# Two stacked attention layers on one core: self attention scores on two 64-row halves with keys spread over half as many columns, value products that alternate between two batches, passes written out

## The chip, the cores and the metric

The kernel runs on one core of one Trainium2 chip. The metric is the device time of one execution in microseconds (us); less is better. Engines are named as in the profile: PE is the matrix engine (PEld its loading of the stationary operand), DVE the vector engine, ACT the scalar engine, POOL the GpSimd engine, SP the engine that issues the transfers. They run side by side and wait for one another on semaphores.

## What is computed

Thirty-two batches of 56 tokens with 128 channels go through two layers. The first has self attention with 16 heads of 8 channels, a cross attention over 1500 context tokens, and an MLP; the second has self attention with 16 heads of 64 channels, and a gated MLP. The change touches the first layer's self attention alone:

```python
def _forward(tgt, src, ...):                 # first layer, T = 56, C = 128, H = 16, HD = 8
    scale = C ** (-0.5)
    x = _layernorm(tgt, ln1_g, ln1_b)
    qkv = x @ sa_wqkv
    q, k, v = (_heads(t) for t in jnp.split(qkv, 3, axis=-1))
    wei = jnp.einsum('bhtd,bhsd->bhts', q, k) * scale
    wei = jnp.where(causal[None, None], wei, NEG_INF)
    wei = jnp.where(tgt_padding_mask[:, None, None, :], NEG_INF, wei)
    wei = jax.nn.softmax(wei, axis=-1)
    sa_out = _merge(jnp.einsum('bhts,bhsd->bhtd', wei, v)) @ sa_wproj + sa_bproj
    result = tgt + sa_out
    ...                                      # cross attention on layernorm(result)
    h = jax.nn.relu(_layernorm(tgt, ln3_g, ln3_b) @ ff_w1 + ff_b1)
    return result + (h @ ff_w2 + ff_b2)
```

## The kernel before

The kernel is one program of three blocks, one behind the other: the self attention of the first layer with its MLP (to about 204 us), the cross attention (to about 970 us), and the second layer. All engines meet at the end of a block. In the first block two batches lie on the 128 partitions, 64 rows each (56 tokens and 8 empty rows): a pair. Sixteen pairs are worked off in four passes of `U = 4` pairs. The passes are a loop that each engine runs for itself (`Fori(0, NIT)`, lines 346, 432, 477 and 539); a wait in it counts semaphores up by the pass, which takes register instructions on the engine.

Within a pass:

- ACT copies the normed inputs to `xn_now` (L434), PE makes queries and keys of all four pairs (L350, L351), the values (L357, two batches by turns on the two halves of the output rows) and the up projection of the MLP (L364); ACT copies the keys to `k0` (L436) and the scaled queries to `q0` (L437), and does the MLP's rectifier (L440).
- Heads have only 8 channels. So that one product makes the scores of many heads, the keys are spread out: `k_wide[u]` has, for each batch of the pair, a column block of 64 keys for each of the 16 heads, and in it the rows of other heads are zero. It is `k0` times `own_head`, a table of ones and zeros, 128x1024 for each batch. DVE makes those of pairs 0 and 1 (L547), POOL those of pairs 2 and 3 (L484). The fourth pair uses the buffer of the first, so POOL waits for the first pair's scores (L481, L482) before it; the third pair uses the buffer `z`, that of the layer norm's rows.
- PE makes the scores of a pair with four products (L379): all 128 rows of the contraction, a batch's 64 queries as the stationary operand, 512 columns of `k_wide`. The two batches go to the two halves of the output rows. The third and fourth pair wait until the maximum over the pair two before is out (`s0_max`), since they use its PSUM banks.
- DVE adds the mask (L559) and takes the maximum (L561), POOL subtracts it (L491), ACT takes the exponential (L445), and DVE the sums (L564). Before the mask add stands the wide form of the values (L553) on DVE.
- PE makes the down projection (L387) ahead of the first transposes of the exponentials (L397); ACT copies the transposed halves to `e0_t` (L451), and `values0` (L325 to L336) multiplies with the values: 16 products for a pair, 8 of the first batch and then 8 of the second, each with 64 stationary columns and 16 moving ones (L330).
- DVE multiplies with the reciprocal sums (L573), PE transposes (L406) and projects (L410), and DVE adds to the residual (L579, L580).

Behind the passes come a layer norm of the result and the queries of the cross attention in two 16-bit parts (`q_halves`, which lies in the buffer of `k_wide[0]`; L587, L589).

## Time and profile before

| | us |
|---|---|
| median of 3 runs | 1343.94 (1338.87 to 1344.26) |
| the profiled execution | 1345.08 |
| its span, first to last instruction | 1343.3 |
| PE busy | 1169.8 (87% of the span) |
| DVE busy | 928.7 (69%) |
| POOL busy | 847.5 (63%) |
| ACT busy | 747.0 (56%) |

Busy shares are means over stages that differ in what bounds them; they say little about one stage.
### The profile page before, as it was taken

How to read it: one execution, taken by the hardware profiler on the slowest of the kernel's cores; microseconds unless marked ns; L12 is line 12 of the kernel's file. 1: busy time of each engine (PE TensorE's matmuls, PEld its weight loads, DVE VectorE, ACT ScalarE, POOL GpSimd, SP SyncE). 2: the span in 40 equal slices, each digit the busy share in tenths (PEclk: the TensorE clock that was granted, in tenths of full speed). 3: DMA queues.
4: the chain of work that ended last, by engine and by line, in shares of the span. 5: the costliest groups of instructions: out<-in, count | busy, mean ns of one | idle time of the engine just before them, and what ended most of it. 6: DMA issues, size and time to landing. Idle time of an engine off the chain costs nothing. (4 is left out here: it accounts for less than half of the span.)

```text
span 1343.3 us, 38339 instructions
## 1 busy us (share of the span) xinstructions
PE 1169.8 (87%) x15980; PEld 795.3 (59%) x15980; DVE 928.7 (69%) x1742; ACT 747.0 (56%) x1029; POOL 847.5 (63%) x1227
## 2 busy tenths in 40 slices
PE   3888855899999999999999999998766887879775
PEld 2555544566666666666666666665443746456472
DVE  6778764777777777778787878777266375674632
ACT  2333333477777777777777777776512435344251
POOL 2455538878787878787888888851028294572830
PEclk9999866899999999999999999999877888989885
DMA  6200003323232323232223232211000000000000
GB/s 170 70 0 0 0 0 108 119 69 107 83 107 69 119 72 114 77 102 89 100 77 112 79 104 86 71 60 37 4 14 1 1 1 10 0 8 2 8 2 7
DMA packets 70398, 75.88 MB, mean 56 GB/s; under 512 B 21308, under 2 KB 64956, under 8 KB 70108
## 3 DMA queue, kind: packets, MB, share of 16 engines
q1 hardware_dynamic: 70236, 73.57, 17.3%
q8 instruction: 120, 1.97, 0.6%
q14 instruction: 42, 0.34, 0.1%
HBM read 32.90 MB, written 0.92 MB: 25 GB/s over the span
## 5 line engine op out<-in xcount | busy, mean ns | idle before, releaser
L928 DVE TENSOR_REDUCE tops_sb<-ps_b 112x2 f32<-112x1000 f32 x384 | 460.4, 1199 | 158.4 <-PE ps_b L778 155.7
L874 ACT ACTIVATE probs_sb<-ps_a 128x896 f32<-128x896 f32 x352 | 322.7, 917 | 118.5 <-PE ps_a L759 118.5
L750 PE MATMUL ps_d<-probs_sb,values_sb 128*32 128x112 f32 x6144 | 229.1, 267 | 0.6 <-ACT probs_sb L874 0.5
L778 PE MATMUL ps_b<-keys_sb,queries_sb 64*112 64x500 f16 x768 | 164.8, 420 | 16.6 <-DVE tops_sb L928 9.8
L217 POOL TENSOR_SCALAR context_sb<-context_sb,ln_sb 125x128 f32<-125x128 f32 x384 | 166.2, 449 | 7.6 <-POOL ln_sb L235 7.5
L750 PEld LDWEIGHTS ps_d<-probs_sb,values_sb 128*32 128x32 f32 x6144 | 135.5, 110 | 40.3 <-issue 7.5
L759 PEld LDWEIGHTS ps_a<-queries_sb,keys_sb 64*128 64x128 f16 x3072 | 125.2, 102 | 48.8 <-ACT probs_sb L874 8.1
L759 PE MATMUL ps_a<-queries_sb,keys_sb 64*128 64x112 f16 x3072 | 141.2, 210 | 4.7 <-ACT probs_sb L874 4.1
L806 PE MATMUL ps_c<-xs_t_sb,w_kv_sb 128*128 128x200 f32 (+1 forms) x384 | 127.4, 430 | 0.0
L815 PE MATMUL ps_c<-w_kv_sb,xs_t_sb 128*128 128x128 f32 x768 | 122.0, 297 | 5.1 <-ACT k_rows_sb L891 5.1
L815 PEld LDWEIGHTS ps_c<-w_kv_sb,xs_t_sb 128*128 128x128 f32 x768 | 97.9, 195 | 27.5 <-issue 21.9
L693 POOL TENSOR_TENSOR k_split_sb<-k_rows_sb,k_split_sb 128x500 f16<-128x500 f32 x96 | 108.8, 1134 | 8.0
L1094 POOL TENSOR_TENSOR turn_b_sb<-turn_b_sb,const_sb 128x448 f32<-128x448 f32 x64 | 62.9, 983 | 75.9 <-DVE turn_b_sb L1429 75.9
L778 PEld LDWEIGHTS ps_b<-keys_sb,queries_sb 64*112 64x112 f16 x768 | 50.6, 126 | 95.7 <-DVE tops_sb L928 70.4
L691 POOL CAST k_split_sb<-k_rows_sb 128x500 f16<-128x500 f32 x96 | 57.5, 599 | 57.8 <-ACT k_rows_sb L891 57.7
L965 DVE BATCH_NORM_STATS2 st_sb<-context_sb 125x6 f32<-125x128 f32 x372 | 87.5, 279 | 2.0 <-POOL ln_sb L235 2.0
L903 ACT ACTIVATE xs_t_sb<-ps_c,cols_sb 128x500 f32<-128x500 f32 x96 | 73.7, 767 | 18.5 <-PE ps_c L828 18.4
L806 PEld LDWEIGHTS ps_c<-xs_t_sb,w_kv_sb 128*128 128x128 f32 x384 | 61.4, 196 | 26.1 <-issue 23.4
L891 ACT COPY k_rows_sb<-ps_c 128x500 f32<-128x500 f32 x96 | 55.3, 576 | 37.9 <-PE ps_c L806 28.2
L233 POOL TENSOR_TENSOR ln_sb<-ln_sb,power_sb 125x12 f32<-125x12 f32 x32 | 72.9, 2279 | 2.5
L206 POOL TENSOR_TENSOR sums_sb<-context_sb 125x768 f32<-125x768 f32 x32 | 58.1, 1817 | 24.4 <-PE ps_d L860 24.4
L896 ACT COPY values_sb<-ps_c 128x512 f32<-128x512 f32 x96 | 56.2, 585 | 29.7 <-PE ps_c L815 29.2
(258 smaller groups left out, 1949.9 us busy)
## 6 DMA issues: line engine op xcount, KB each, us to landing
keys_sb<-k_split_sb SPq DMA_DIRECT2D x288, 125.0 KB, 2.5
context_sb<-in_ctx SPq DMA_DIRECT2D x32, 750.0 KB
queries_sb<-q_split_sb SPq DMA_DIRECT2D x24, 112.0 KB, 5.6
keys_sb<-in_ones SPq DMA_DIRECT2D x3, 375.0 KB, 4.5
w_qk_sb<-in_w_qkv SPq DMA_DIRECT2D x1, 1024.0 KB, 12.3
queries_sb<-shift_sb SPq DMA_DIRECT2D x64, 1.8 KB
x_all_sb<-in_x SPq DMA_DIRECT2D x2, 448.0 KB
queries_sb<-in_zeros SPq DMA_DIRECT2D x8, 112.0 KB, 5.5
```

Source lines behind the costliest of these rows:

```text
L217: ins = nc.gpsimd.tensor_scalar(tile, tile, ln[:, 4, k:k + 1], ln[:, 5, k:k + 1], ALU.mult, ALU.add)
L233: link(nc.gpsimd.tensor_tensor(rstd, var, power[:].broadcast_to([KP, KT]), ALU.pow))
L693: nc.gpsimd.tensor_tensor(k_split[:, 1, k_slice], k_rows[(b + u) % 2][:], k_split[:, 0, k_slice], ALU.subtract).then_inc(Q["klow_ready"], 1)
L750: last = nc.tensor.matmul(o_bank[32 * (g % 4):32 * (g % 4) + 32, 112 * (g // 4):112 * (g // 4) + 112], values[r][:, k, g, :], probs[k % 2] ...
L759: last = nc.tensor.matmul(ps_a[:, 512 * e + GN * g:512 * e + GN * g + GN], keys[r][64 * e:64 * e + 64, g, KEY * k:KEY * k + KEY], queries_ ...
L778: last = nc.tensor.matmul(ps_b[0:2 * T, 512 * e:512 * e + 500], queries_of(b + d, e, g), keys[(r + d) % 3][64 * e:64 * e + 64, g, 500 * u: ...
L806: last = nc.tensor.matmul(ring_of(b, u)[:, lo:hi], w_kv[:, 0:128], xs_t[:, 500 * u + lo:500 * u + hi], start=True, stop=True)
L815: last = nc.tensor.matmul(ring_of(b, 3 + u)[:, 128 * k:128 * k + 128], xs_t[:, 4 * KEY * u + KEY * k:4 * KEY * u + KEY * k + KEY], w_kv[:, ...
L874: nc.scalar.activation(probs[s % 2][:].rearrange("p (e n) -> p e n", e=2), halves(ps_a[:, :]), ACT.Exp).then_inc(Q["probs_ready"], 1)
L903: nc.scalar.activation(xs_t[:, 500 * u:500 * u + 500], ring_of(b, 6 + u)[:, 0:500], ACT.Identity, bias=cols[:, 3:4], scale=cols[:, 2:3]).t ...
L928: nc.vector.tensor_reduce(tops[(b + d) % 2][:, :, n // 3, n % 3], ps_b[0:2 * T, :].rearrange("p (e n) -> p e n", e=2)[:, :, 0:500], axis=A ...
L965: ins = nc.vector.bn_stats(st[:, k, :], context[(r + 1) % 3][:, k, :])
```

## The change

The 128 rows of the contraction hold 16 heads of 8 channels, so the upper 64 rows hold heads 0 to 7 and the lower 64 rows heads 8 to 15. Now a score product contracts over 64 rows only, and a column block of `k_wide` serves two heads: head h in the upper half of the rows and head h + 8 in the lower half. `own_head` and `k_wide` have 8 column blocks instead of 16. A pair still has four products of 512 columns; the first half's go to the first PSUM bank, the second half's to the second, as the heads did before.

The buffers that were shared are now separate: four `k_wide`, and `q_halves`. With that POOL's wait for the first scores goes. In `values0` the loop over the two batches is inside that over the head groups. The passes are Python loops now, so each engine's four passes are written out and the waits compare with constants.

```diff
-    own_head = (p[:, None] // D0 == np.arange(H0)[None]).astype(np.float32)
+    own_head = (p[:, None] % 64 // D0 == np.arange(H0 // 2)[None]).astype(np.float32)
...
-            k_bufs = [sb1(f"k_wide{n}", [128, 2, H0, TP])[:] for n in range(2)]
-            k_bufs.append(z[:].rearrange("p n c -> p (n c)").rearrange("p (b h s) -> p b h s", b=2, h=H0))
-            k_wide = [k_bufs[n] for n in (0, 1, 2, 0)]
+            k_wide = [sb1(f"k_wide{n}", [128, 2, H0 // 2, TP]) for n in range(U)]
...
-            q_halves = k_bufs[0].rearrange("p b h s -> p (b h s)").bitcast(F16).rearrange(
-                "p (q a n) -> p q a n", q=NPAIR // U, a=2)
+            q_halves = sb1("q_halves", [128, NPAIR // U, 2, U * 128], F16)
...
                     def values0(pe, i, u):
...
-                        for b2 in range(2):
-                            for c in range(8):
+                        for c in range(8):
+                            for b2 in range(2):
                                 last = nc.tensor.matmul(banks[0][64 * b2:64 * b2 + 64, 128 * u + 16 * c:128 * u + 16 * c + 16],
...
-                    with pe.Fori(0, NIT) as i:
+                    for i in range(NIT):
...
-                            for half in range(2):
-                                for b2 in range(2):
+                            for b2 in range(2):
+                                for half in range(2):
+                                    rows = slice(64 * half, 64 * half + 64)
                                     last = nc.tensor.matmul(ps[64 * b2:64 * b2 + 64, 512 * half:512 * half + 512],
-                                                            q0[:, 128 * u + 64 * b2:128 * u + 64 * b2 + 64],
-                                                            k_wide[u][:, b2, 8 * half:8 * half + 8, :].rearrange("p h s -> p (h s)"),
+                                                            q0[rows, 128 * u + 64 * b2:128 * u + 64 * b2 + 64],
+                                                            k_wide[u][rows, b2, :, :].rearrange("p h s -> p (h s)"),
                                                             start=True, stop=True)
...
                         for u in (2, 3):
-                            if u == 3:
-                                wait("s0_done", 1)
                             for b2 in range(2):
                                 ins = nc.gpsimd.tensor_tensor(
                                     k_wide[u][:, b2, :, :],
-                                    k0[:, 128 * u + 64 * b2:128 * u + 64 * b2 + 64].unsqueeze(1).broadcast_to([128, H0, TP]),
-                                    own_head.unsqueeze(2).broadcast_to([128, H0, TP]), ALU.mult)
+                                    k0[:, 128 * u + 64 * b2:128 * u + 64 * b2 + 64].unsqueeze(1).broadcast_to([128, H0 // 2, TP]),
+                                    own_head.unsqueeze(2).broadcast_to([128, H0 // 2, TP]), ALU.mult)
...
```

DVE's product at L547 changes in the same way, and the loops of ACT, POOL and DVE as PE's.

What stands on POOL in a pass before, from the wide keys of pairs 2 and 3 (written to `z` and `k_wide`) to the first subtraction of the maximum (`s_0`):

```order
L484 ISA
L484 TENSOR_TENSOR z_sb<-k_sb,const_sb 128x1024 [waits self_k0_ready]
L484 TENSOR_TENSOR z_sb<-k_sb,const_sb 128x1024
L283 ISA
L484 TENSOR_TENSOR k_wide_sb<-k_sb,const_sb 128x1024 [waits self_s0_done]
L484 TENSOR_TENSOR k_wide_sb<-k_sb,const_sb 128x1024
L491 TENSOR_TENSOR s_0_sb<-s_0_sb,s_max_sb 128x1024 [waits self_s0_max]
```

And the same place now:

```order
L480 ISA
L480 TENSOR_TENSOR k_wide_sb<-k_sb,const_sb 128x512 [waits self_k0_ready,x_loaded]
L480 TENSOR_TENSOR k_wide_sb<-k_sb,const_sb 128x512 x3
L487 TENSOR_TENSOR s_0_sb<-s_0_sb,s_max_sb 128x1024 [waits self_s0_max]
```

The four products stand in one row without a wait between them, each half as wide, and the register instructions are gone.

On PE, the scores of the first three pairs before (`self_k_ready` and `self_k_later` are the wide keys of DVE and POOL, `self_up_ready` the rectifier on ACT):

```order
L283 ISA [waits self_q0_ready]
L379 MATMUL ps_a<-k_wide_sb,q_sb 64x512 [waits self_k_ready]
L379 MATMUL ps_a<-k_wide_sb,q_sb 64x512 x3
L283 REGISTER_ALU
L283 REGISTER_ALU [waits self_k_ready]
L379 MATMUL ps_c<-k_wide_sb,q_sb 64x512 [waits self_up_ready]
L379 MATMUL ps_c<-k_wide_sb,q_sb 64x512 x3
L379 MATMUL ps_a<-z_sb,q_sb 64x512 [waits self_s0_max,self_k_later]
```

And now:

```order
L377 MATMUL ps_a<-k_wide_sb,q_sb 64x512 [waits self_k_ready,self_q0_ready]
L377 MATMUL ps_a<-k_wide_sb,q_sb 64x512 x3
L377 MATMUL ps_c<-k_wide_sb,q_sb 64x512 [waits self_up_ready,self_k_ready]
L377 MATMUL ps_c<-k_wide_sb,q_sb 64x512 x3
L377 MATMUL ps_a<-k_wide_sb,q_sb 64x512 [waits self_s0_max,self_k_later]
```

As many products stand there, in the same place and with the same waits; they contract over half as many rows, and the third pair's keys no longer lie in `z`.

## Rows read from the trace of the kernel before

**Rows 1.** Stretch of the third pass: start:end, length, busy time (records) by engine, PEclk, DMA

```profile
100.80:138.70 37.90, 32.95 (x280) 21.92 (x280) 27.79 (x24) 13.64 (x21) 18.01 (x8) 0.95 0.00 0
```

**Rows 2.** Timeline (start, duration, engine, line, operation, [idle before <-releaser]): block's end

```profile
202.86 1.09 DVE L589 TENSOR_TENSOR q_split_sb<-k_wide_sb,const_sb 128x896 f16<-128x896 f16 x1
...
204.47 0.37 PE L860 MATMUL ps_d<-ones_sb,sums_sb 125*128 125x1 f32 x1 [5.65 <-DVE xs_t_sb L909]
```

**Rows 3.** Timelines of DVE and POOL, third pass, wide keys one by one

```profile
105.97 1.23 DVE L547 TENSOR_TENSOR k_wide_sb<-k_sb,const_sb 128x1024 f32<-128x1024 f32 x1 [1.44 <-ACT k_sb L436]
106.01 2.94 POOL L484 TENSOR_TENSOR z_sb<-k_sb,const_sb 128x1024 f32<-128x1024 f32 x1 [17.24 <-ACT k_sb L436]
107.11 2.92 DVE L547 TENSOR_TENSOR k_wide_sb<-k_sb,const_sb 128x1024 f32<-128x1024 f32 x1
...
112.80 1.21 DVE L547 TENSOR_TENSOR k_wide_sb<-k_sb,const_sb 128x1024 f32<-128x1024 f32 x1
112.99 2.78 POOL L484 TENSOR_TENSOR k_wide_sb<-k_sb,const_sb 128x1024 f32<-128x1024 f32 x1 [1.20 <-PE ps_a L379]
```

**Rows 4.** Two lines' instructions: count, ns min/median/max, first and last start us

```profile
L567 DVE TENSOR_TENSOR r_sb<-x_all_sb,rows_sb x4: 691/692/869, 54.2 to 169.4; 128x512 f32 x4
...
L1094 POOL TENSOR_TENSOR turn_b_sb<-turn_b_sb,const_sb x64: 973/982/993, 999.5 to 1267.0; 128x448 f32<-128x448 f32 x64
```

**Rows 5.** Timeline of PE, third pass, up projection to value products

```profile
107.14 3.89 PE L364 MATMUL ps_c<-xn_now_sb,w_up_sb 128*128 128x512 f32 x8
110.96 1.94 PE L379 MATMUL ps_a<-k_wide_sb,q_sb 128*64 128x512 f32 x8
...
120.06 1.94 PE L379 MATMUL ps_c<-k_wide_sb,q_sb 128*64 128x512 f32 x8 [0.45 <-DVE s_max_sb L561]
...
125.60 0.60 PE L397 MATMUL ps_b<-const_sb,s_sb 128*128 128x128 f32 x4
...
130.22 0.60 PE L397 MATMUL ps_d<-const_sb,s_sb 128*128 128x128 f32 x4
130.75 1.83 PE L330 MATMUL ps_a<-v_wide_sb,e_t_sb 128*64 128x16 f32 x32
132.51 0.66 PE L397 MATMUL ps_b<-const_sb,s_sb 128*128 128x128 f32 x4
...
133.53 3.29 PE L330 MATMUL ps_a<-v_wide_sb,e_t_sb 128*64 128x16 f32 x64
```

**Rows 6.** Timeline of DVE, third pass: first mask add, last sum, normalising

```profile
115.07 1.21 DVE L559 TENSOR_TENSOR s_sb<-ps_a,mask_sb 128x1024 f32<-128x1024 f32 x1
...
128.30 1.22 DVE L564 TENSOR_REDUCE s_sum_sb<-s_sb 128x16 f32<-128x1024 f32 x1 [0.24 <-ACT s_sb L445]
...
136.85 0.69 DVE L573 TENSOR_TENSOR q_sb<-ps_a,s_sum_sb 128x512 f32<-128x512 f32 x1 [4.44 <-PE ps_a L330]
```

**Rows 7.** Timelines of POOL and ACT, third pass, around the fourth exponential

```profile
124.76 1.91 POOL L491 TENSOR_TENSOR s_sb<-s_sb,s_max_sb 128x1024 f32<-128x1024 f32 x1 [0.48 <-DVE s_max_sb L561]
...
126.24 0.58 ACT L451 COPY e_t_sb<-ps_b 128x512 f32<-128x512 f32 x1 [0.87 <-PE ps_b L397]
...
127.19 1.07 ACT L445 ACTIVATE s_sb<-s_sb 128x1024 f32<-128x1024 f32 x1
128.15 0.59 ACT L451 COPY e_t_sb<-ps_b 128x512 f32<-128x512 f32 x1
```

**Rows 8.** Timeline of PE in the second attention: two score products, weighted values

```profile
1037.41 1.25 PE L1224 MATMUL ps_a<-k_sb,q_sb 64*64 64x73 f32 x32
...
1039.20 0.74 PE L1224 MATMUL ps_b<-k_sb,q_sb 64*64 64x73 f32 x32
...
1050.33 2.08 PE L1245 MATMUL ps_c<-e_t_sb,v_sb 73*64 73x64 f32 x64
```

**Rows 9.** Stretches, columns as rows 1: end of the second pass; second attention's scores

```profile
100.60:104.00 3.40, 2.97 (x10) 2.45 (x11) 0.76 (x2) 1.32 (x2) 0.00 (x0) 0.51 0.00 0
...
1022.60:1040.00 17.40, 11.99 (x273) 7.73 (x272) 11.21 (x18) 4.10 (x6) 13.29 (x13) 0.71 0.01 2
```

More of the change, by code:

```diff
@@ L60, in constants @@
     return np.ascontiguousarray(table.astype(np.float32))
-CONST_WIDTH = 128 + 16 + 2 + 2 + 64 + NK1 + 64 + 64 + 1
+CONST_WIDTH = 128 + 8 + 2 + 2 + 64 + NK1 + 64 + 64 + 1
 def program(nc, dram):
@@ L86, in program @@
         ident = const[:, at:at + 128]; at += 128
-        own_head = const[:, at:at + 16]; at += 16
+        own_head = const[:, at:at + 8]; at += 8
         own_in_pair = const[:, at:at + 2]; at += 2
@@ L431, in _ @@
                     act.wait_ge(A["xn3_ready"], NIT)
-                    with act.Fori(0, NIT) as i:
+                    for i in range(NIT):
                         wait = waiter1(act, i)
@@ L476, in _ @@
                     pool.wait_ge(x_loaded, 48)
-                    with pool.Fori(0, NIT) as i:
+                    for i in range(NIT):
                         wait = waiter1(pool, i)
@@ L538, in _ @@
                     ins.then_inc(Q["st_ready"], 1)
-                    with ve.Fori(0, NIT) as i:
+                    for i in range(NIT):
                         wait = waiter1(ve, i)
@@ L548, in _ @@
                                     k_wide[u][:, b2, :, :],
-                                    k0[:, 128 * u + 64 * b2:128 * u + 64 * b2 + 64].unsqueeze(1).broadcast_to([128, H0, TP]),
-                                    own_head.unsqueeze(2).broadcast_to([128, H0, TP]), ALU.mult)
+                                    k0[:, 128 * u + 64 * b2:128 * u + 64 * b2 + 64].unsqueeze(1).broadcast_to([128, H0 // 2, TP]),
+                                    own_head.unsqueeze(2).broadcast_to([128, H0 // 2, TP]), ALU.mult)
                             ins.then_inc(S["k_ready"], 1)
```

## Prediction

> **What bounds the kernel now.** I first read the stretch by passes: the changed code is the loop of four passes of the self attention, and one pass, the third, takes 37.90 us [rows 1]; the others look alike. Does a shorter loop shorten the kernel? The next block's first product on PE starts after the last instruction of this block's DVE has ended, and nothing in between waits for a transfer [rows 2], so what the four passes lose, the span loses; the stages behind are not touched.
>
> Inside a pass I followed one pass (the third) on the engines' timelines, asking at each step who was waited for. Three things in a row set it.
>
> First the wide key rows. Between 105.97 and 114.01 DVE makes four products of 128x1024, and they take 8.04 us because POOL makes its own at the same time and the two take turns: the 1.23 us of the first is a product alone, the second lasts 2.92, and POOL's first lasts 2.94 [rows 3]. Behind them, on the same queue, stand the wide values and then the first mask add at 115.07 [rows 6].
>
> Second the chain DVE mask add and maximum, POOL subtraction, ACT exponential. It has a steady step per pair, and the diff leaves its instructions alone; it is moved as a whole. Its end is POOL's fourth subtraction, 124.76 plus 1.91 [rows 7].
>
> Third the tail on PE: the down projection, transposes, ACT copies, and the value products of four pairs. DVE sits idle 4.44 us for the last of these before it can normalise at 136.85 [rows 6]. ACT's copies there wait for PE, not the other way round.
>
> **The change part by part.** All for one pass, at the third's times.
>
> *Key rows.* Each product now covers 512 columns. Of the 1024 wide, the part that excludes the other engine is, for DVE, 107.11+2.92 less 106.01+2.94, so 1.08; for POOL, 106.01+2.94 less 105.97+1.23, so 1.75 [rows 3]. Half of the first is about 0.55, and a single 512-wide DVE product alone has 0.69 [rows 4]. For POOL half would be 0.88; a 448-wide one of its products lasts 0.98 [rows 4], so I take 0.95. By turns: 0.69 + 3x0.55 + 3x0.95 = 5.19 against 8.04, so 2.85 less. If every product costs its full record, 4x0.69 + 3x0.98 = 5.70, it is 2.34 less. If POOL did not get in the way at all, PE would be next: the first score product starts at 110.96 behind the MLP's up projection, and with 1.08 for it (below) DVE could start its mask add at 112.04 instead of 115.07; so no more than 3.03. I take 2.85: the mask add starts at 112.22, just behind what PE allows.
>
> POOL's wait for the first scores, before its second pair of rows (the idle 1.20 at 112.99 [rows 3]), goes. POOL's four products then end near 112.2; the third pair's scores want them only when the first maximum is out, after 114, so this wait is worth nothing by itself; its absence puts POOL's work into DVE's way three times instead of twice, which the sum above counts.
>
> *Scores.* Eight records of 512 columns took 1.94 where the up projection's eight, with the same columns, took 3.89 [rows 5]: the two batches already ran side by side. Now there are four quadrants. The nearest row is the second attention's score product, also 64 rows by 64 columns and also by quadrants: 32 records of 73 columns in 0.74 [rows 8], 23 ns each, where 73/512 of a 512-column step of about 0.43 would be 61 ns. So four do run side by side, and 1.94 loses two of its four steps: 1.08. Bounds: 1.94 (no overlap of the row halves) and 1.08. On the path it counts once, at the fourth pair, whose product is straight ahead of the down projection: 0.86. At the others DVE is busy longer than PE.
>
> *Value products.* 32 records took 1.83, 57 ns each [rows 5]. The nearest row is the second attention's weighted values, with as wide a stationary operand, alternating between the column halves: 64 records in 2.08, 32.5 ns each [rows 8]. So 1.04 instead of 1.83 for a pair, and 2.08 instead of 3.29 for the last two. Bounds: 1.83 (nothing) and half, 0.92.
>
> The Trainium skill has a rule that speaks against this part: "TensorE: Matmul & The Clock Gate", Part 3 (Packing small matmuls), says that a weight load overlaps with products in flight only where the row groups differ, and here only the column groups do. By it the value products would stay at 1.83; the 32.5 ns above speak against it, and I count it as a rival below.
>
> *The tail, put together.* The fourth score product starts 2.85 earlier, at 117.21. From it to the first transposes were 5.54 with the down projection between; less 0.86 that is 4.68, so they start at 121.89 (was 125.60). ACT copies the first pair at 122.53 (was 126.24) and is done with it when POOL's fourth subtraction ends at 126.67 less 2.85, so the fourth exponential starts at 123.87 (was 127.19, held up by the copies) [rows 5, 7]. The second pair's copies follow 0.96 later [rows 7], 124.83, and end near 125.9. They now end last: the third pair's transposes need their banks, where before they stood behind the first value products. From 125.95: 0.53 to the second value products (130.75 less 130.22), 1.04 for these, 1.02 to get through the fourth transposes (133.53 less 132.51 [rows 5]), then two value products in 2.08: 130.62, and DVE follows 0.03 later, 130.65 instead of 136.85. DVE's idle time there shrinks from 4.44 by 2.88 (6.20 of the end less 3.32 of the fourth exponential) to 1.6, so DVE's sums, the last of which waits for that exponential [rows 6], still hide. A pass loses **6.2 us**, four passes 24.8.
>
> *Unrolling.* Waits become constants and the branch at a pass's end goes. The branch and register work lies where the engine waits for ACT or PE anyway (DVE 1.44 idle ahead of its first product [rows 3]); I take zero. Fresh instructions must be fetched for each pass instead of a loop body; the stages behind are all straight-line code already and PE's and DVE's rows there follow one another, so zero too, with 1 us either way in the range.
>
> *PE's clock.* Once in a pass the granted clock falls to its lower level: 0.51 over 3.40 us, after PE had done narrow value products and waited for DVE [rows 9]; over a pass it averages 0.95 [rows 1]. With scores at 1.08 in the same step of the chain, PE has longer gaps. A stretch like this one costs half of its 3.40, 1.7, if PE's work there ends last. Between none and one more in every pass I take one and a half in all four: 2.6 us.
>
> Sum: 24.8 - 2.6 = 22.2. The profiled execution took 1345.08 us (span 1343.3), 1.1 over the median 1343.94 of runs from 1338.87 to 1344.26. Against its own time that is 1322.9, against the median **1322**.
>
> **The rivals.**
> *The value products don't overlap* (weight loading stays serial). Then key rows and scores remain: 2.85 + 0.86, and 24.8 falls to 4x3.7 = 14.8: 1329. Against it stand the 32.5 ns [rows 8]. Chance 0.08.
>
> *The clock takes back a large part.* In the second attention, where PE has short score bursts with gaps, the mean clock is 0.71 over 17.40 us [rows 9], and the same 32 records take 1.25 instead of 0.74 [rows 8]. If each pass gets one more low stretch and every second pass two, 6x1.7 = 10.2 goes: 1343.94 - 14.6 = 1329.3. For it: the scores now are such bursts. Against it: the down projection behind them is dense, and a mean of 0.95 over a pass leaves room for one low stretch only [rows 1]. Chance 0.2.
>
> The Trainium skill, "TensorE: Matmul & The Clock Gate", Part 1, says that PE is throttled by default and that activity releases it; an idler PE is thus at risk. The rows agree that it falls after little work; what these bursts do no row of this loop shows.
>
> *Slower.* If the clock stays low from the scores to the end of the value products, all of PE's tail runs at half speed. The point from which this decides: a low stretch over 2x6.2 = 12.4 us longer per pass eats the gain. From 117 to 130 there is room for 13 at most of work as now planned, which at half speed takes up to 11 us more: 5 us a pass slower, 1364. Dense work raised the clock within a pass each time so far. Chance 0.03.
>
> *No change that shows* (the change doesn't reach the end, something behind absorbs it): speaks against it that the next block starts on the last instruction [rows 2]. Chance 0.02, time 1342.
>
> *More gain*: no further low stretch, and half a us a pass because waits are cheaper as constants: 24.8 + 2 = 27, 1317. Chance 0.12.
>
> **How the numbers follow.** Forecast 0.55, rivals 0.08, 0.2, 0.03, 0.02, 0.12. The time is the likeliest case's, 1322. The range takes in the gain case and run-to-run spread below (1314) and the first two rivals above (1332). Faster by over 0.5% (about what a measurement here can tell from no change) 0.95, same 0.02, slower 0.03.
>
> **What would show it.** The mask add of each pass starts some 6.2 us after DVE's first key row (9.1 before); a score product lasts 1.1 (1.94), value products 1.0 to 1.1 (1.83); DVE's wait before normalising is 1.6 (4.44); a pass takes 31 to 32.5 us (37.90). The prediction is wrong if value products keep 1.8, if the granted clock of a pass is clearly under 0.95, or if POOL's half-width products don't halve.

## The result, and the profile after

The changed kernel took 1319.76 us (median of 4 runs, 1319.39 to 1320.74) against 1342.37 us (4 runs, 1338.87 to 1344.26) beside it: a ratio of 0.983, interval 0.981 to 0.985, so 22.6 us faster. The prediction of 1322 and its range hold. The profiled execution took 1320.03 us, with a span of 1318.2. The sum behind the number was less good than the number, as the rows show. Lines of the changed kernel are two to four lower than in the kernel before (L543 was L547, L377 was L379).

The four passes of the changed kernel, from one first key row of DVE to the next (the last row ends at the normalising); columns as in [rows 1]:

```profile
30.70:62.70 32.00, 27.00 (x288) 18.21 (x284) 24.82 (x25) 13.88 (x22) 13.43 (x9) 0.95 0.28 85
62.70:96.80 34.10, 28.48 (x284) 18.77 (x282) 25.65 (x24) 13.68 (x21) 13.00 (x9) 0.90 0.01 2
96.80:130.90 34.10, 28.48 (x284) 18.76 (x282) 25.65 (x24) 13.67 (x21) 12.99 (x8) 0.90 0.00 1
130.90:158.00 27.10, 22.63 (x256) 14.88 (x250) 23.95 (x22) 11.50 (x17) 20.67 (x20) 0.94 0.00 1
```

The first pass is as predicted (31 to 32.5); the second and third take 34.10, at a granted clock of 0.90. PE's timeline of the third pass, from the four score products to the last value product, where [rows 5] had 1.94, 1.83 and 3.29:

```profile
101.74 1.09 PE L377 MATMUL ps_a<-k_wide_sb,q_sb 64*64 64x512 f32 x8
102.79 1.09 PE L377 MATMUL ps_c<-k_wide_sb,q_sb 64*64 64x512 f32 x8
106.40 1.09 PE L377 MATMUL ps_a<-k_wide_sb,q_sb 64*64 64x512 f32 x8 [2.52 <-DVE s_max_sb L557]
108.78 1.99 PE L377 MATMUL ps_c<-k_wide_sb,q_sb 64*64 64x512 f32 x8 [1.30 <-DVE s_max_sb L557]
110.70 4.48 PE L385 MATMUL ps_d<-w_down_sb,up_sb 128*128 128x128 f32 x32
...
117.38 1.11 PE L327 MATMUL ps_a<-v_wide_sb,e_t_sb 128*64 128x16 f32 x32
...
121.50 2.04 PE L327 MATMUL ps_a<-v_wide_sb,e_t_sb 128*64 128x16 f32 x64
```

The sizes of the products are those of the prediction, except that the fourth score product takes 1.99 and the down projection behind it 4.48. In the first pass the same two took 1.09 and 3.84, and PE's wait before the third pair's scores was shorter, 1.75 instead of 2.52:

```profile
39.56 1.09 PE L377 MATMUL ps_a<-k_wide_sb,q_sb 64*64 64x512 f32 x8 [1.75 <-DVE s_max_sb L557]
41.95 1.09 PE L377 MATMUL ps_c<-k_wide_sb,q_sb 64*64 64x512 f32 x8 [1.29 <-DVE s_max_sb L557]
42.97 3.84 PE L385 MATMUL ps_d<-w_down_sb,up_sb 128*128 128x128 f32 x32
```

The first key row of DVE and of POOL, in the first pass and then in the third (compare [rows 3]), and all four of DVE in the third with its first mask add and its normalising (compare [rows 6]):

```profile
30.75 0.69 DVE L543 TENSOR_TENSOR k_wide_sb<-k_sb,const_sb 128x512 f32<-128x512 f32 x1
30.86 1.48 POOL L480 TENSOR_TENSOR k_wide_sb<-k_sb,const_sb 128x512 f32<-128x512 f32 x1 [25.62 <-ACT k_sb L434]
...
96.82 1.57 DVE L543 TENSOR_TENSOR k_wide_sb<-k_sb,const_sb 128x512 f32<-128x512 f32 x1 [1.86 <-ACT k_sb L434]
96.80 1.04 POOL L480 TENSOR_TENSOR k_wide_sb<-k_sb,const_sb 128x512 f32<-128x512 f32 x1 [15.50 <-ACT k_sb L434]
...
96.82 5.91 DVE L543 TENSOR_TENSOR k_wide_sb<-k_sb,const_sb 128x512 f32<-128x512 f32 x4 [1.86 <-ACT k_sb L434]
...
103.79 1.21 DVE L555 TENSOR_TENSOR s_sb<-ps_a,mask_sb 128x1024 f32<-128x1024 f32 x1
...
123.60 0.69 DVE L569 TENSOR_TENSOR q_sb<-ps_a,s_sum_sb 128x512 f32<-128x512 f32 x1 [1.90 <-PE ps_a L327]
```

In the first pass DVE starts first, and its four rows last 5.04. In the third POOL starts 0.02 earlier, DVE's first row lasts 1.57 instead of 0.69, and the four last 5.91; the second and fourth pass are alike.

The block ends with the last part of the split queries (before 203.95, [rows 2]), at 184.97:

```profile
183.88 1.09 DVE L585 TENSOR_TENSOR q_split_sb<-q_halves_sb,const_sb 128x896 f16<-128x896 f16 x1
```

So the changed block gives 18.98 us of the 25.05 between the two profiled executions (1345.08 less 1320.03). The other 6.1 come from code that the change does not touch. The last block, from the last maximum of the cross attention on, before and then after, as table rows like those above:

```profile
945.20:1343.30 398.10, 304.63 (x3453) 212.91 (x3447) 209.26 (x519) 151.43 (x210) 188.21 (x162) 0.85 0.02 5
...
925.40:1318.20 392.80, 296.46 (x3455) 207.28 (x3449) 208.87 (x519) 151.33 (x210) 188.23 (x162) 0.89 0.02 5
```

The same work takes 398.1 us at a mean clock of 0.85 and 392.8 at 0.89. Two questions follow: why three of four passes fall 2.1 us short of the first, and what the last block's 5.3 us have to do with the change.

### The profile page after: what moved, and what is told of

Its sections match the earlier page's. It is cut to its first block and busy times, and to the rows that moved or that the text cites. A ratio compares the mean times of both kernels' runs of the same rounds, so it can differ in the third digit from the quotient of the medians.

```text
span 1318.2 us, 38111 instructions
## 1 busy us (share of the span) xinstructions
PE 1137.9 (86%) x15980; PEld 773.6 (59%) x15980; DVE 918.8 (70%) x1742; ACT 747.0 (57%) x1029; POOL 828.4 (63%) x1227
## 3 DMA queue, kind: packets, MB, share of 16 engines
q8 instruction: 127, 2.08, 0.7%
## 5 line engine op out<-in xcount | busy, mean ns | idle before, releaser
L899 ACT ACTIVATE xs_t_sb<-ps_c,cols_sb 128x500 f32<-128x500 f32 x96 | 73.7, 767 | 18.5 <-PE ps_c L824 18.4
```

What stands on the lines that cost most here:

```text
L899: nc.scalar.activation(xs_t[:, 500 * u:500 * u + 500], ring_of(b, 6 + u)[:, 0:500], ACT.Identity, bias=cols[:, 3:4], scale=cols[:, 2:3]).t ...
```

## The experiments

The theory after this reading had two parts. Passes 2 to 4 lose 0.8 us because POOL takes the first turn, and 1.3 because the clock is low at the fourth scores and the down projection. The rivals: that writing the passes out costs time by itself, that the parts of the change pay less than their sum, and that the last block's gain is made by the changed passes.

What each kernel's profile and times gave. "Rows" is the time of DVE's four key rows in the third pass; "to norm." runs from the first of them to the normalising and "gap" from there to the next pass's first key row, both the median of the values in the trace; "end" is the end of the first block in us from the start of the span; "last" is the last block; "profiled" is the time of the execution that these come from. The ratio is to the kernel before on the same chip.

| kernel | rows | to norm. | gap | end | last | profiled us | median us (lowest to highest) | ratio, interval |
|---|---|---|---|---|---|---|---|---|
| before | 8.04 | 30.9 | 7.3 | 203.95 | 398.1 | 1345.08 | 1342.37 (1338.87 to 1344.26) | |
| changed | 5.91 | 26.8 | 7.3 | 184.97 | 392.8 | 1320.03 | 1319.76 (1319.39 to 1320.74) | 0.983 (0.981 to 0.985) |
| a1_first_turn | 5.04 | 25.3 | 7.3 | 181.85 | 398.2 | 1322.11 | 1320.42 (1313.82 to 1324.41) | 0.982 (0.977 to 0.986) |
| a2_filler | 5.91 | 25.4 | 8.6 | 184.25 | 398.3 | 1324.55 | 1312.60 (1310.83 to 1324.55) | 0.977 (0.975 to 0.980) |
| a3_values_back | 5.91 | 29.7 | 8.0 | 200.95 | 392.8 | 1336.06 | 1336.06 (1331.50 to 1344.19) | 0.995 (0.991 to 0.999) |
| a4_rows_back | 11.48 | 31.7 | 7.4 | 204.15 | 398.4 | 1344.68 | 1338.53 (1334.30 to 1344.68) | 0.996 (0.994 to 0.998) |
| a5_again | 5.91 | 26.8 | 7.3 | 185.57 | 392.8 | 1320.64 | 1320.11 (1319.22 to 1321.95) | 0.984 (0.981 to 0.987) |
| b2_unrolled | 8.07 | 30.9 | 8.0 | 203.91 | 398.2 | 1344.29 | 1344.92 (1343.85 to 1347.55) | 1.002 (1.001 to 1.004) |
| b4_values_only | 8.04 | 28.2 | 7.3 | 192.47 | 395.7 | 1330.28 | 1327.78 (1324.58 to 1332.91) | 0.989 (0.985 to 0.994) |
| b3_pool_late | 2.50 | 24.6 | 7.3 | 179.49 | 394.7 | 1315.70 | 1318.93 (1314.02 to 1324.29) | 0.985 (0.979 to 0.990) |
| c4_fillers | 5.91 | 25.4 | 5.8 | 176.68 | 392.3 | 1311.81 | 1310.72 (1310.22 to 1311.81) | 0.977 (0.973 to 0.982) |
| c3_late_fillers | 2.50 | 24.6 | 5.8 | 171.86 | 392.5 | 1305.91 | 1310.80 (1305.91 to 1313.47) | 0.977 (0.974 to 0.981) |
| d1_delay | 5.91 | 27.2 | 5.7 | 186.02 | 394.8 | 1323.04 | 1322.68 (1320.47 to 1323.04) | 0.986 (0.981 to 0.990) |
| d3_wide_late | 4.63 | 26.7 | 5.7 | 184.27 | 398.8 | 1325.28 | 1322.97 (1318.74 to 1326.01) | 0.986 (0.981 to 0.991) |

Since the last block alone differs by up to 6.5 us between kernels that share its code, the columns on the first block decide in what follows, not the medians; they come from one execution each. How far such an end can be trusted shows in `changed` and `a5_again`, the same kernel: 184.97 and 185.57.

### The parts of the change

**b2_unrolled**: the kernel before, its passes written out. The four loops (L346, L432, L477, L539) change alike:

```diff
-                    with ve.Fori(0, NIT) as i:
+                    for i in range(NIT):
```

> The kernel before, with its four passes written out and nothing else changed. Prediction's step: worth zero, 1 us either way, first block's end 203 to 205, a pass 37.9. Rival, from the two waits that stand ahead of DVE's first key product once the waits are constants: POOL takes the first turn, key rows last about 1 us more in passes 2 to 4 (9.0 instead of 8.04), first block's end near 207, about 1347.

The block ends at 203.91 (203.95): nothing, as predicted. The rival was half right. DVE's and POOL's first key rows in the third pass, and all four of DVE:

```profile
108.17 2.96 DVE L547 TENSOR_TENSOR k_wide_sb<-k_sb,const_sb 128x1024 f32<-128x1024 f32 x1 [2.06 <-ACT k_sb L436]
108.15 1.90 POOL L484 TENSOR_TENSOR z_sb<-k_sb,const_sb 128x1024 f32<-128x1024 f32 x1 [18.28 <-ACT k_sb L436]
...
108.17 8.07 DVE L547 TENSOR_TENSOR k_wide_sb<-k_sb,const_sb 128x1024 f32<-128x1024 f32 x4 [2.06 <-ACT k_sb L436]
```

Written out, POOL does take the first turn, where in the loop it came 0.04 behind DVE [rows 3]. But it costs 0.03 here, because POOL stops after two rows to wait for the first scores: it stands in DVE's way twice, whoever begins.

**b4_values_only**: the kernel before, and in `values0`

```diff
-                        for b2 in range(2):
-                            for c in range(8):
+                        for c in range(8):
+                            for b2 in range(2):
```

> The kernel before, with its loop of passes, and only the value products in alternating order. Prediction's step: a product of 32 takes 1.04 to 1.11 instead of 1.83, the last two 2.08 instead of 3.29; normalising comes about 2.5 us earlier per pass (0.8 for the second pair's, 1.2 for the last two, some of it in the copies), four passes about 8 to 10 us: first block's end near 195, about 1334. Rival, that the parts pay only together, because half as fast scores leave DVE's sums last: the wait before normalising shrinks by under 1 us per pass, first block's end above 200, 1340 or more.

PE's value products of the third pass:

```profile
123.99 1.11 PE L330 MATMUL ps_a<-v_wide_sb,e_t_sb 128*64 128x16 f32 x32
...
126.06 1.11 PE L330 MATMUL ps_a<-v_wide_sb,e_t_sb 128*64 128x16 f32 x32
...
128.12 2.04 PE L330 MATMUL ps_a<-v_wide_sb,e_t_sb 128*64 128x16 f32 x64
```

Normalising comes 2.7 us earlier in a pass (28.2 instead of 30.9), and the block ends 11.5 earlier. The order of two loops is thus worth more than half of the change's 19.0 in this block, and more than expected (an end near 195). In the trace the loads and products of the two column halves now start in pairs, under 0.01 us apart, where before one half's eight followed the other's. The rival that the parts pay only together falls for this part.

**a3_values_back**: the changed kernel with that order undone (the diff above reversed).

> The changed kernel with the old order of the value products (8 of one batch, then 8 of the other). Theory (alternating lets weight loads of the two column halves overlap, and the tail is PE's): value products 1.83 instead of 1.11 for a pair and 3.3 instead of 2.04 for the last two, DVE's wait before normalising longer by some 2.5 us, a pass longer by 2.5: 1329.6. Rival (ACT's copies bound the tail, alternating is worth only the last two products): 1.3 a pass, 1325.

The block ends at 200.95, 16.0 later: more than the 11.5, and the median of 1336.06 is above both numbers expected. Normalising comes 2.9 to 3.0 later in passes 2 to 4 and 5.0 later in the first, against the 2.5 of the theory, for beside the products the clock went. The fourth scores, the down projection and the last value products of the third pass:

```profile
117.71 1.89 PE L377 MATMUL ps_c<-k_wide_sb,q_sb 64*64 64x512 f32 x8 [1.30 <-DVE s_max_sb L557]
119.53 4.65 PE L385 MATMUL ps_d<-w_down_sb,up_sb 128*128 128x128 f32 x32
...
131.95 3.44 PE L327 MATMUL ps_a<-v_wide_sb,e_t_sb 128*64 128x16 f32 x64
```

The low stretch before the down projection is here in the first pass too, and the mean clocks of the first three passes are 0.89, 0.82 and 0.86 (0.95, 0.90 and 0.90 in the changed kernel).

**a4_rows_back**: the changed kernel with keys 1024 wide and 128-row scores, but with the separate buffers, the passes written out and the new order of the value products.

```diff
-            k_wide = [sb1(f"k_wide{n}", [128, 2, H0 // 2, TP]) for n in range(U)]
+            k_wide = [sb1(f"k_wide{n}", [128, 2, H0, TP]) for n in range(U)]
...
-                                                            q0[rows, 128 * u + 64 * b2:128 * u + 64 * b2 + 64],
+                                                            q0[:, 128 * u + 64 * b2:128 * u + 64 * b2 + 64],
```

> The changed kernel with the scores on all 128 rows and keys spread over 16 column blocks again, in four buffers of their own; loops written out and alternating value products stay. Theory: DVE's four key products and POOL's four, each 1024 wide, take turns all the way: 1.23 + 3x(1.75+1.08) = 9.7, and 1.75 more where POOL starts first, against 5.0 and 5.9; so about 5 us a pass more: 1340. With it the score products take 1.94 and the clock stays up between them, so the fourth of them and the down projection lose nothing against the changed kernel. Rival (the four quadrants matter, the narrower keys not): 0.9 to 1.5 a pass, 1324.

The block ends at 204.15. Against `b4_values_only` (192.47) this kernel has the passes written out, which alone gives nothing, and POOL's wait for the first scores gone. That costs all that the value products gave:

```profile
107.48 11.48 DVE L542 TENSOR_TENSOR k_wide_sb<-k_sb,const_sb 128x1024 f32<-128x1024 f32 x4 [2.81 <-ACT k_sb L433]
...
107.46 10.42 POOL L479 TENSOR_TENSOR k_wide_sb<-k_sb,const_sb 128x1024 f32<-128x1024 f32 x4 [15.89 <-ACT k_sb L433]
```

Without its break POOL stands in the way of each of DVE's four rows: 11.48 instead of 8.04, and 9.75 in the first pass, where DVE begins (expected: 9.7, and 1.75 more where POOL begins). Three times 3.44 and once 1.71 is 12.0, and the two ends differ by 11.7.

**d3_wide_late**: `a4_rows_back`, with POOL starting behind DVE's rows (the edit of `b3_pool_late` below).

> The changed kernel with the full-width key rows and scores of before (1024 columns, 128 rows, a buffer for each pair), and POOL's rows behind DVE's. It asks what the halved columns are worth once the two engines do not take turns. If nearly all of the 5.6 us that the full-width rows cost in turns was POOL's getting in the way: DVE's rows 4.9, first mask add 7.0 behind the first row, normalising 28 to 29 (scores 1.94 and later rows of POOL), first block's end 187 to 192. If POOL's late wide rows (about 7 us) now hold up the third pair's scores: normalising 31 or later, first block's end 199 or more.

```profile
97.89 4.63 DVE L542 TENSOR_TENSOR k_wide_sb<-k_sb,const_sb 128x1024 f32<-128x1024 f32 x4 [2.81 <-ACT k_sb L433]
...
105.12 1.22 DVE L554 TENSOR_TENSOR s_sb<-ps_a,mask_sb 128x1024 f32<-128x1024 f32 x1 [1.46 <-PE ps_a L376]
...
102.60 7.48 POOL L479 TENSOR_TENSOR k_wide_sb<-k_sb,const_sb 128x1024 f32<-128x1024 f32 x4 [20.06 <-DVE k_wide_sb L542]
```

Alone, DVE needs 4.63 for full-width rows, and the block ends at 184.27, no later than the changed kernel's: better than either theory's number. With the turns out of the way the halved columns and their scores bring normalising 2.1 us earlier in a pass (26.7 less the 24.6 of `b3_pool_late`), 8.6 in four. The block's ends are only 4.8 apart, mainly since the gaps of `d3_wide_late` came out 3.4 shorter in sum (5.7 twice, where the clock stayed up). With the turns, the same halving is worth 19.2 (`a4_rows_back` 204.15, changed 184.97). So more than half of what it does in the change is to make a collision cheaper that the change itself made worse by taking POOL's wait away.

### The passes that fall short

**a1_first_turn**: an increment of a semaphore at the end of DVE's pass, so that DVE's wait for its own last step hangs on that instruction and not on the next pass's first key row.

```diff
                         link(nc.vector.tensor_tensor(x4, banks[3].rearrange("p (u c) -> p u c", u=U), x4, ALU.add))
+                        alone(ve)
                         ends()
```

> The changed kernel with one empty DVE instruction at a pass's end, which takes up DVE's wait for its own last add, so that the first wide key product of the next pass waits for the keys alone. Theory (who starts first matters): in passes 2 to 4 of the changed kernel POOL's first product started 0.02 us ahead of DVE's and took the first turn; here DVE starts first as in pass 1, the four key products take 5.0 instead of 5.9 us in all passes, the mask add comes 6.2 instead of 7.0 behind the first, and three passes save 0.8 each: 1317.4. Rival (POOL's four products simply cost this much, pass 1 was short for another reason): 5.9 stays in passes 2 to 4, time as the changed kernel, 1319.8.

```profile
95.83 0.69 DVE L543 TENSOR_TENSOR k_wide_sb<-k_sb,const_sb 128x512 f32<-128x512 f32 x1 [2.29 <-ACT k_sb L434]
95.87 1.55 POOL L480 TENSOR_TENSOR k_wide_sb<-k_sb,const_sb 128x512 f32<-128x512 f32 x1 [15.62 <-ACT k_sb L434]
...
95.83 5.04 DVE L543 TENSOR_TENSOR k_wide_sb<-k_sb,const_sb 128x512 f32<-128x512 f32 x4 [2.29 <-ACT k_sb L434]
```

DVE has the first turn again, by 0.04, and its rows take 5.04 in passes 2 to 4. So it was the second wait that gave POOL the first turn. The mask add comes 6.15 behind the first key row in passes 2 and 3, 0.8 earlier, as the theory said, and 6.50 in pass 4, where it waited for PE: 2.1 us in three passes. The block ends 3.1 earlier, but the clock's falls lie elsewhere in this execution (the down projection takes 4.94, 3.84 and 5.58 in passes 2 to 4), so what the rows gave of the 3.1 beyond these 2.1 cannot be told from it. The total of 1317.4 did not come: the four runs spread from 1313.82 to 1324.41, and the last block takes 398.2 in the profiled one.

**a2_filler**: products into a PSUM bank that nobody reads any more in that pass, two before the third pair's scores and one before the fourth's, while PE waits for DVE.

```diff
                             if u >= 2:
+                                for _ in range(4 - u):
+                                    nc.tensor.matmul(banks[2], w_qkv0[:, 128:256], xn1, start=True, stop=True)
                                 wait("s0_max", u - 1)
```

> The changed kernel with idle PE time filled: two 128x512 products, whose result nobody reads, ahead of the third pair's wait for the maximum, and one ahead of the fourth's. Theory (gaps between the shorter score products let the clock fall): with the gaps filled the clock stays up, the fourth score product takes 1.1 instead of 2.0 and the down projection 3.85 instead of 4.5 in passes 2 to 4; each saves about 1.4: 1315.5. Rival (the clock falls there whatever PE does, or the fall costs nothing since ACT and DVE end last): the products keep 2.0 and 4.5, or the passes keep 34.1 us: 1319.8, or up to 1 us a pass slower where the fillers stand in the way, 1324.

The fourth scores and the down projection of the third pass, and then the head of the next pass:

```profile
109.82 1.09 PE L379 MATMUL ps_c<-k_wide_sb,q_sb 64*64 64x512 f32 x8 [0.24 <-DVE s_max_sb L559]
110.84 3.84 PE L387 MATMUL ps_d<-w_down_sb,up_sb 128*128 128x128 f32 x32
...
127.64 1.91 PE L347 MATMUL ps_a<-xn_now_sb,w_qkv_sb 128*128 128x512 f32 x2
129.35 1.91 PE L348 MATMUL ps_b<-xn_now_sb,w_qkv_sb 128*128 128x512 f32 x2
```

With PE busy in those gaps both products are at full speed, and normalising comes 1.34 earlier. But the queries and keys at the pass's head now take 1.91 each (1.83 and 1.02 in the changed kernel): the low stretch has moved there, the gap grows from 7.3 to 8.6, and the mean clock of the second and third pass stays at 0.90. The block gains 0.7 in this execution, little more than the 0.6 by which the two traces of the changed kernel differ. It was the slowest of the five (1324.55 at a mean clock of 0.926 over the whole run; the other four 1310.83 to 1315.83 at 0.940 to 0.947). These have no trace, and they are faster by 8.7 to 13.7 us, more than the last block's 6, so in them the low stretch probably did not move there; that is argued, not shown.

**b3_pool_late**: POOL waits for DVE's rows instead of for the keys.

```diff
-                        wait("k0_ready")
+                        wait("k_ready", 2)
                         for u in (2, 3):
```

> The changed kernel, with one thing moved: POOL starts its key rows only behind DVE's, which have the first turn and are alone. Theory: DVE's four rows last 2.5 instead of 5.9, the first mask add comes 6.1 behind the first key row (now PE is what it waits for) instead of 6.97, normalising 25.9 instead of 26.8, the gap behind it stays 7.3; first block's end 181 to 182.5. Rival (POOL's rows, now later, hold up the third pair's scores): first key row to normalising as before or longer, first block's end 185 or more. The total moves by the last stage as well, if that goes over to its longer form (398 instead of 393): 1316 or 1322.

```profile
96.32 2.50 DVE L543 TENSOR_TENSOR k_wide_sb<-k_sb,const_sb 128x512 f32<-128x512 f32 x4 [2.78 <-ACT k_sb L434]
...
102.40 1.23 DVE L555 TENSOR_TENSOR s_sb<-ps_a,mask_sb 128x1024 f32<-128x1024 f32 x1 [2.44 <-PE ps_a L377]
```

DVE's rows take 2.50, but the mask add comes only 0.9 earlier, for now it waits 2.44 for PE's first scores. That is the limit that the prediction's bound of 3.03 named. Beyond the theory, which had normalising at 25.9, the clock's share at the scores came back too: the fourth scores take 1.09 and the down projection 3.84, normalising stands at 24.6 to 24.7 in all four passes, and a low stretch is left at the end of a pass (gap 8.6 once). The block gains 5.5. PE waits 1.75 before the third scores here, as in the changed kernel's first pass, and not 2.52: a later mask add makes that wait longer. In the traces of kernels with halved keys and without added products (changed, `a5_again`, `a1_first_turn`, `a3_values_back`, `d1_delay` and this one) the clock fell at the scores in all 12 passes with a wait of 2.52, and in 4 of the 12 with 1.75. So part of the clock's loss probably follows from POOL's first turn; that the longer wait is the cause is argued from this count, not shown.

**c4_fillers**: products as in `a2_filler` (of weights alone), and two more where PE waits for the normalising and for ACT's copy behind it.

```diff
                         values0(pe, i, U - 1).then_inc(S["o0_done"], 1)
+                        nc.tensor.matmul(banks[2], w_qkv0[:, 128:256], w_up0[:], start=True, stop=True)
                         wait("o0_ready")
...
+                        nc.tensor.matmul(banks[2][:, 0:256], w_qkv0[:, 128:256], w_up0[:, 0:256], start=True, stop=True)
                         wait("o0t_ready")
```

> The changed kernel with the products into an unused bank alone (before the third and fourth pair's scores, and before the two last waits of a pass), POOL as in the changed kernel. If the clock is what the rest of the shortfall is made of: key rows stay at 5.9, first key row to normalising 25.4, gap behind it 5.8 instead of 7.3, first block's end 174 to 176, total 1310 to 1315. If the gain of the version with both came from POOL's later start and the clock only followed: gap 7.3 to 8.6, first block's end above 181.

Its second pass, in the columns of the passes above:

```profile
62.40:93.60 31.20, 29.63 (x295) 18.45 (x293) 25.56 (x25) 13.70 (x21) 12.99 (x9) 1.00 0.01 2
```

The clock stays at its upper level, the pass takes 31.2 instead of 34.1, the gap 5.8 instead of 7.3, and the block ends 8.3 earlier, at 176.68 (174 to 176 expected). Both parts of the clock's loss are thus shown, and the part in the gap was there before the change as well ([rows 9]: 0.51 over 3.40). The Trainium skill ("TensorE: Matmul & The Clock Gate", Part 1) says that the low clock is the default and activity releases it; this run agrees, with 1.00 against 0.90.

**c3_late_fillers**: the edits of `b3_pool_late` and `c4_fillers` together.

> The changed kernel with three additions: POOL starts its key rows behind both key blocks, so that DVE has the first turn; products into an unused bank before the third and fourth pair's scores; and one each before the two last waits of a pass on PE, to keep its clock up where it fell. Theory (passes 2 to 4 lose 2.1 us to POOL's first turn and to the clock): key rows back to about 5.0, the fourth score product 1.1 and the down projection 3.85, first key row to normalising 24 to 25 instead of 26.8, the gap behind it 7.3, first block's end 176 to 179, total 1310 to 1318 by the last stage's length. Rival (the added products stand in the way of PE's own, or the clock falls in another place instead): normalising earlier, the gap behind it longer by as much, first block's end 183 to 186.

```profile
61.20:91.50 30.30, 29.43 (x294) 18.46 (x292) 22.24 (x24) 13.68 (x21) 11.65 (x8) 1.00 0.01 2
```

A pass of 30.3 us, with DVE's rows at 2.50 instead of the expected 5.0, and the block ends at 171.86, 13.1 earlier (5.5 and 8.3 alone; 176 to 179 expected). Both kernels with products in all gaps are faster than the changed one, by 9 us in the median; the slowest run of either took 1313.47, the fastest of the changed kernel 1319.22. Between the two the medians do not decide, since `c3_late_fillers` spreads over 7.6 us.

### The last block

**a5_again**: the changed kernel, no edit.

> The changed kernel once more, as a yardstick for the others on the same chip. If the passes always fall in with the clock in the same way, every run is between 1319 and 1321, as the first four were, and the last stage of the profile takes 392.8 us. If the last stage's length is settled anew in each run (392.8 or 398.2 in the kernels so far), the runs spread over 1319 to 1325. First block's end near 185 by both.

Its last block takes 392.8 again, and all eight runs of this kernel lie between 1319.2 and 1322.0 (1319 to 1321 expected, if the clock falls in the same way each time).

**d1_delay**: one more sum behind the last pass.

```diff
+                    nc.vector.reduce_sum(s_sum[:, 0, 0:8], s0[0][:, 0:8, :], AX.X)
                     ve.sem_inc(A["r1_ready"], 1)
```

> The changed kernel with one more sum over 512 columns on DVE behind the last pass, whose result nobody uses: it delays all that follows by about 0.6 us and changes nothing else. Theory, that the last stage's length (392.8 in both profiles of the changed kernel, 398.2 in most others) hangs on the time at which it starts against the clock's turns: it goes to 398, total 1325 to 1326.5. Rival, that it hangs on something in the changed passes: 392.8 as before, total 1320.5 to 1321.5.

The last block of this run:

```profile
926.50:1321.20 394.70, 298.29 (x3453) 208.39 (x3447) 208.99 (x519) 151.32 (x210) 188.45 (x162) 0.87 0.02 5
```

Neither number came: 394.8 from the last maximum's own start (the row starts 0.04 later), between the two. Nor was the delay all that differed. The clock fell at other places in the passes of this run (normalising 27.6 and 28.2 behind the first key row in passes 1 and 2, gaps of 5.7), though the delay stands behind them, and the block ended 1.0 later than the changed kernel's instead of 0.6. What holds: this block takes 392.3 to 398.8 us in kernels that do not differ in it, shorter at a higher clock. It does not go by when the first block ends: `a3_values_back` has 392.8 with an end at 200.95, `a1_first_turn` 398.2 with 181.85. What remains open is which of these lengths goes with which kernel, and whether the changed kernel falls into the short one by its passes or by chance of when it arrives.

## Why the prediction was right, and where its sum was not

The total was right partly by luck: two errors cancelled. The block gave 19.0 where the sum said 22.2; the rest gave 3.6 in the medians (22.6 less 19.0; 6.1 in the profiled pair) where the sum had nothing.

- **Scores and value products** were as sized: 1.09 (predicted 1.08), 1.11 and 2.04 (1.04 and 2.08). The 2.5 us a pass that the value products have in the sum (6.2 less 3.7) measured 2.7 alone (`b4_values_only`). The rival that weight loads stay serial falls: 32 records in 1.11 instead of 1.83, in a kernel where only their order changed. With that the rule of the Trainium skill ("TensorE: Matmul & The Clock Gate", Part 3), that a load overlaps only where the row groups differ, does not hold here.
- **The tail put together** was right for the first pass: mask add 6.19 behind the first key row (6.25 in the sum), normalising 24.67 behind it, so 6.2 less than 30.88, as written, and DVE's wait before it 1.57 (1.6).
- **Key rows** are the term that was mis-sized in the other three passes. 0.69 + 3x0.55 + 3x0.95 supposed that DVE has the first turn. Written out, POOL has it: 5.91 instead of 5.04, and the mask add comes 6.97 behind the first key row, 0.8 later; 2.3 over three passes. "Unrolling: zero" holds alone (`b2_unrolled`), and so the sum missed that the missing POOL wait turns the new first turn into a fourth one.
- **PE's clock** took 1.34 in each of three passes (normalising 26.77 against `a2_filler`'s 25.43), 4.0 us, where the sum had 2.6. The sum had one and a half low stretches more in four passes, at 1.7 each; there were three, at 1.34 each, and the size lay between the sum and the rival's 10.2. The place was as told, and so was the mechanism as far as it goes: with the gaps filled the clock stays up (`c4_fillers`, 1.00). But a gap alone does not settle it, for the first pass and `b3_pool_late` have the same wait of 1.3 before the fourth scores and no fall there; and the sum took this term and the key rows' as independent, which the longer wait behind POOL's first turn speaks against.
- Together: 24.8 - 2.3 - 4.0 = 18.5, and 0.5 from the first pass's start, the gaps and the stages behind, gives the 19.0.
- **What lies behind the block** was taken as fixed. It shifts with the block, but its own clock is not fixed: 398.1 and 392.8 for the last block. The prediction used the 1338.87 to 1344.26 of the runs before as spread and did not ask which stage made it. The 36 runs of the kernel before, on several chips, spread further, from 1336.69 to 1347.15, while the changed kernel's eight stay within 2.8: which length of the last block the kernel before meets how often, and so how much of the 3.6 belongs to the change, no run settles.

One of its own signs that it would be wrong, a clock clearly under 0.95, did appear (0.90), and the second and third pass took 34.1 instead of 31 to 32.5.

## What to carry to other kernels

When a wait is taken away, ask what the freed engine will collide with: here POOL's wait had kept it out of DVE's way, and its loss cost full-width rows 12 us, more than the 8.6 that halving them saved once the collision was gone. A gap that keeps PE waiting can cost more than itself where dense work follows it (here 1.34 on the fourth scores and the down projection); products that fill one gap can push the low clock into the next, as in the traced execution of `a2_filler`, so look at every gap of the loop. And judge an edit by the end of the stage it is in before the total: a stage behind, untouched, moved by up to 6.5 us.

## What was not expected of the hardware

DVE and POOL do not always take strict turns. In the first pass of `a1_first_turn` POOL's first key row starts 0.02 before DVE's, and yet DVE makes all four of its rows at full speed while POOL's one lasts 3.41 (1.04 alone):

```profile
31.03 2.49 DVE L543 TENSOR_TENSOR k_wide_sb<-k_sb,const_sb 128x512 f32<-128x512 f32 x4
...
31.01 3.41 POOL L480 TENSOR_TENSOR k_wide_sb<-k_sb,const_sb 128x512 f32<-128x512 f32 x1 [25.76 <-ACT k_sb L434]
```

The Trainium skill ("SBUF — State Buffer", SBUF: two separate sides) says that the two share a pair of ports, which whoever starts first holds for its whole instruction while the other blocks. That an engine blocks for the other's product agrees with the rows here, but for about 0.15 us at its edges ([rows 3]: 1.08 of DVE's 1.23 and 1.75 of POOL's 1.90 came behind the other's end); that the one that starts first goes first, these two starts do not show, for POOL's is the earlier and DVE goes first; no run was made for it.
